# Value products of two attention heads issued alternately, in their own groups of 32 output columns

## The reference, cut to what matters

```python
attn = softmax(q @ k.T * scale + bias)        # per head, 256 x 256
out = jnp.einsum('bqk,bkd->bqd', attn, v)     # per head, 256 x 16: the value product
out = out.reshape(...) @ proj_w + proj_b
```

## Time and profile before

| | us |
|---|---|
| median of 3 runs | 290.22 |
| lowest and highest | 287.61, 291.16 |
| span of the profiled execution, first to last instruction | 287.2 |
| PE busy in it | 241.8 (84%) |
| DVE busy | 106.3 (37%) |
| ACT busy | 78.7 (27%) |
| POOL busy | 25.3 (9%) |

### The profile page before, as it was taken

One profiled execution on the slowest core, in us unless ns is written; L12 is line 12 of the kernel. 1 busy time (PEld: TensorE's weight loads), 2 busy tenths in 40 slices (PEclk: granted clock), 3 DMA queues, 4 the chain that ended last, 5 costly groups with the idle time before them and its releaser, 6 DMA issues.

```text
span 287.2 us, 3244 instructions
## 1 busy us (share of the span) xinstructions
PE 241.8 (84%) x1255; PEld 149.7 (52%) x1266; DVE 106.3 (37%) x262; ACT 78.7 (27%) x156; POOL 25.3 (9%) x45
## 2 busy tenths in 40 slices
PE   7856069999899579999989874999999877499995
PEld 2754046555357256655466443665564762375552
DVE  4566034324638133424311522321125651334222
ACT  2581003432030002342252200224321470023431
POOL 7510812601000000000000000000000000000000
PEclk9975557999999955999999996589999977658999
DMA  6999959409003900000000093000000089200000
GB/s 171 236 153 133 123 139 308 69 3 110 2 1 51 113 0 0 2 0 2 0 0 0 3 124 40 0 0 2 0 0 2 27 109 118 21 0 0 0 3 27
DMA packets 10574, 15.06 MB, mean 52 GB/s; under 512 B 2912, under 2 KB 7296, under 8 KB 10528
## 3 DMA queue, kind: packets, MB, share of 16 engines
q1 hardware_dynamic: 7472, 12.63, 28.0%
q0 software_dynamic: 3088, 2.24, 6.3%
HBM read 8.30 MB, written 0.20 MB: 30 GB/s over the span
## 4 chain that ended last, share of the span: by engine, by line
PE 63%; DMA 15%; DVE 7%; ACT 7%; issue 5%; SPq 2%; DVEq 0%; ACTq 0%
PE PC L940 15%; DMA QS<-RL 9%; PE RING L922 8%; PE RING L879 8%; PE RING L923 6%; DMA QS<-QL 4%; PE PB L960 4%; PE RING L824 4%; PE PC L951 2%; DMA RELT<-in_relt 2%; PE PC L865 2%; PE RING L1111 2%; PE PA L1117 2%; PE PC L943 2%; PE PB L824 1%
## 5 line engine op out<-in xcount | busy, mean ns | idle before, releaser
L738 DVE TENSOR_REDUCE NM<-RING 128x2 fp32r<-128x512 f32 (+1 forms) x48 | 30.8, 658 | 73.9 <-PE RING L879 73.5
L879 PE MATMUL RING<-KS,QS 128*128 128x256 f32 (+1 forms) x96 | 28.4, 404 | 28.2 <-DMA QS<-RL 17.4
L824 PE MATMUL RING<-WARM 128*128 128x512 bf16 x195 | 50.0, 401 | 2.3 <-POOL WARM L343 1.3
L940 PE MATMUL PC<-PR,VX 128*32 128x256 f32 x192 | 47.6, 395 | 0.0
L506 ACT ACTIVATE PR<-RING 128x512 f32<-128x512 f32 x48 | 28.6, 595 | 43.0 <-PE RING L923 42.5
L879 PEld LDWEIGHTS RING<-KS,QS 128*128 128x128 f32 x96 | 20.6, 268 | 36.2 <-issue 33.5
L922 PE MATMUL RING<-QS,KS 128*128 128x256 f32 x96 | 34.3, 374 | 0.3
L824 PEld LDWEIGHTS RING<-WARM 128*128 128x128 bf16 x206 | 20.9, 104 | 25.5 <-issue 4.9
L923 PE MATMUL RING<-MT,SELM 128*128 128x256 f32 (+1 forms) x96 | 30.4, 332 | 0.0
L922 PEld LDWEIGHTS RING<-QS,KS 128*128 128x128 f32 x96 | 20.3, 212 | 16.1 <-issue 10.6
L940 PEld LDWEIGHTS PC<-PR,VX 128*32 128x32 f32 x192 | 16.5, 111 | 17.3 <-issue 3.2
(11 more groups left out here) (153 smaller groups left out, 262.8 us busy)
## 6 DMA issues: line engine op xcount, KB each, us to landing
KS<-KH SPq DMA_DIRECT2D x8, 192.0 KB, 6.8
WQKV<-in_w SPq DMA_DIRECT2D x2, 576.0 KB, 7.2
WO<-in_wo SPq DMA_DIRECT2D x4, 288.0 KB, 9.1
W<-in_ff SPq DMA_DIRECT2D x2, 576.0 KB, 7.6
WQKV<-in_w SPq DMA_DIRECT2D x2, 432.0 KB, 6.6
KS<-in_hot POOLq DMA_DIRECT2D x1, 768.0 KB, 15.4
QS<-QHL SPq DMA_DIRECT2D x2, 384.0 KB, 11.4
KS<-KL SPq DMA_DIRECT2D x4, 192.0 KB, 8.6
```

Source lines behind the costliest of these rows:

```text
L738: V.tensor_reduce(NM[g % 2][:, :, h % GH], slot("m", l, h)[:, 0:2 * n_keys].rearrange("p (q k) -> p q k", q=2), AX.X, ALU.max, negate=True ...
L824: M(bank, WARM[:, 0:P], WARM[:, :], start=True, stop=True)
L879: ins = M(s[:, q * n_keys:(q + 1) * n_keys], QS[l % 2][:, h, q * P:(q + 1) * P], KS[:, h, keys], start=True, stop=True)
L940: ins = M(dst, VX[:, k, h, :], PR[:, h % NPR, k * T:(k + 1) * T], start=(k == 0), stop=(k == 1 and l != 2))
```

## The change

`values` takes two heads. It waits for both heads' probabilities and then issues, for each half of the keys, the matmul of the first head and that of the second; the two heads write different groups of 32 partitions of the same PSUM buffer. The loop calls it at odd `h` from 3 on, for heads `h - 3` and `h - 2`, and once at the end for heads 10 and 11. The number of matmuls is the same, and each does the same work. The other lines of the diff remove empty lines, so line numbers are smaller in the changed kernel (L940 is L897, L922 and L923 are L874 and L875, L879 is L831).

```diff
-            def values(l, h):
+            def values(l, first):
 
-                g, j = h // GH, h % GH
-                pe.wait_ge(*upto("probs", l, h + 1))
-                if h == 0:
+                g = first // GH
+                heads = range(first, first + 2)
+                pe.wait_ge(*upto("probs", l, first + 2))
+                if first == 0:
...
-                dst = PC[g % 2][32 * j:32 * j + 32, 0:T]
+                def columns(h):
+                    return PC[g % 2][32 * (h % GH):32 * (h % GH) + 32, 0:T]
+
                 for k in range(2):
-                    ins = M(dst, VX[:, k, h, :], PR[:, h % NPR, k * T:(k + 1) * T], start=(k == 0),
-                            stop=(k == 1 and l != 2))
+                    for h in heads:
+                        ins = M(columns(h), VX[:, k, h, :], PR[:, h % NPR, k * T:(k + 1) * T], start=(k == 0),
+                                stop=(k == 1 and l != 2))
+                        if k == 1 and l != 2:
+                            ins.then_inc(sem("pv"), 1)
                 if l == 2:
-                    ins = M(dst, VR[:, h, :], PG[g % 2][:, :], start=False, stop=True)
-                ins.then_inc(sem("pv"), 1)
+                    for h in heads:
+                        M(columns(h), VR[:, h, :], PG[g % 2][:, :], start=False, stop=True).then_inc(sem("pv"), 1)
...
-                    if h >= 2:
-                        values(l, h - 2)
+                    if h >= 3 and h % 2:
+                        values(l, h - 3)
...
                 values(l, NH - 2)
-                values(l, NH - 1)
                 out_project(l, 0)
```

More of the change, by code:

```diff
@@ L933, in values @@
                         pe.wait_ge(sem("vr"), 1 + 2 * GH)
-                if j == 0 and g >= 2:
+                if first % GH == 0 and g >= 2:
                     pe.wait_ge(*upto("o", l, g - 1))
-                if j == 0 and l == 2:
+                if first % GH == 0 and l == 2:
                     pe.wait_ge(*upto("reg probs", l, g + 1))
-                dst = PC[g % 2][32 * j:32 * j + 32, 0:T]
+                def columns(h):
+                    return PC[g % 2][32 * (h % GH):32 * (h % GH) + 32, 0:T]
                 for k in range(2):
-                    ins = M(dst, VX[:, k, h, :], PR[:, h % NPR, k * T:(k + 1) * T], start=(k == 0),
-                            stop=(k == 1 and l != 2))
+                    for h in heads:
[3 more added lines that the diff above has]
+                            ins.then_inc(sem("pv"), 1)
                 if l == 2:
-                    ins = M(dst, VR[:, h, :], PG[g % 2][:, :], start=False, stop=True)
-                ins.then_inc(sem("pv"), 1)
+                    for h in heads:
+                        M(columns(h), VR[:, h, :], PG[g % 2][:, :], start=False, stop=True).then_inc(sem("pv"), 1)
             def row_sums(l, g):
```

## The result

| | before | changed |
|---|---|---|
| median, us | 289.22 (4 runs) | 269.11 (4 runs) |
| lowest and highest | 287.61, 291.16 | 267.03, 271.20 |
| span of the profiled execution | 287.2 | 269.4 |
| PE busy in it | 241.8 (84%) | 222.9 (83%) |

The ratio is 0.928, 95% interval 0.922 to 0.933: 20 to 21 us faster, inside the range of 261 to 273 us and 2 us above the forecast of 267.0. Medians and low-clock means in this document are over all runs of a kernel, ratios and their intervals leave out runs more than 1.5% above their kernel's fastest. The profiled execution of the changed kernel was the longest of the four (271.2 us), so its trace shows the losses a little large.

The account below looks back on a forecast made before the run. TensorE was taken to bound the attention loop. Gains of 16.4 us (layers 0, 1, 3) and 6.85 (layer 2), 23.2 in total, took the span from 287.2 to 264.0; 3.0 us more gave 267.0, range 261 to 273.

Parts of the forecast that it names:

- TensorE bounds the loop: Attention loop: the other engines wait for TensorE; over two heads, 3.30 us, PE is busy throughout, ACT 1.19 us.
- A pair costs one product: Two value products in different groups of 32 output columns run side by side: 1.00 us, against 0.98 for one.
- the first pair: Start of each loop, heads 0 and 1 moved behind head 3: gain 0.95 us, not 1.6, DVE being late next.
- The beat of two heads: Two heads in mid-loop, layers 0, 1 and 3: 2.14 us instead of 3.30, gain 1.16 us, three times per layer.
- The end of the loop: Scores of head 10 to `out_project`, 4.74 us before: gain 1.0 to 1.2 us, taken as 1.0.
- Layer 2: Six-row value products: two heads take 2.56 us instead of 4.15, the end gains 1.45; whole layer 6.85 us.
- the sum: Gains added over the loops: 5.45 us each in layers 0, 1 and 3, 6.85 in layer 2, total 23.2 us.
- The clock: Rise from 1.2 to 2.4 GHz in every loop: moments shift, no mean change, 1.5 us to either side.
- rival 1: Clock rises one 3.4 us stretch later: 1.7 us lost per layer, 6.8 in all four, 273.8 us; chance 0.10.
- my signs of being wrong: Five steps in a pair, PE waiting for L506 between scores, or a later clock rise behind a loop's start.

Follow-up runs that it names:

- the filler: Changed kernel with three matmuls on zeros per layer where the value product of head 0 had stood, behind `for_maxima(7)`; 265.65 us, ratio 0.918.

## Why the prediction was right, and which term was off

**TensorE bounds the loop: right.** L897 waits 0.0 us, ACT still sits idle 32 us behind the scores.

**A pair costs one product: right.** Forecast 1.00 us, measured 0.98. The evidence for it, heads 9 and 10 of the kernel before, was also enough to say that the alternation isn't what does it; the run without alternation confirms that, and the one with shared columns shows that without the overlap there is no gain. That holds at the full clock: in layers 1 to 3 the first pair still fell into the low clock, and in layer 1 it took 1.85 us (111.01 to 112.86).

**The beat of two heads: right.** 2.14 us forecast and measured. At head 6 (53.29 to 56.07) it is 2.78 us, no wait for ACT.

**The first pair: right in mechanism, right in size in layer 0 alone.** DVE was late next, as said: TensorE stood 0.36 us, where I had 0.5. Scores of head 2 to scores of head 4 took 4.76 us (46.16 to 50.92) against 5.92 (45.86 to 51.78), a gain of 1.16 where 0.95 stood, part of it a clock that rose some 0.6 us sooner behind these scores (at 48.4 against 48.7). I took the same for the other loops, whose timelines had the same shape; there the stretch became 0.45 to 1.18 us longer, by the clock.

**The end of the loop: right.** From the scores of head 10 to `out_project` 3.72 us (58.21 to 61.93) against 4.74, gain 1.02 for a forecast of 1.0. The profile shows the two blocks of the end:

```profile
59.93 2.06 PE L897 MATMUL PC<-PR,VX 128*32 128x256 f32 x16
...
60.30 0.58 ACT L461 ACTIVATE PR<-RING 128x512 f32<-128x512 f32 x1
...
61.93 0.46 PE L919 MATMUL PB<-O,WO 128*96 128x256 f32 x1
```

**Layer 2: right from head 4 on.** Its end took 4.15 us (196.23 to 200.38), as forecast, instead of 5.60, and from head 4 to `out_project` the gain is 6.08 us, where the sum has 5.95. The layer as a whole gave 5.20 for 6.85, by the stretch ahead of head 4.

**The clock: this term was wrong.** I took "no mean change, 1.5 us to either side". It was 10 us more at the low level per run, of 269 (85 against 75). Over the four windows above, 12.4 us more went with a loss of 5.1 us, 0.41 us for each; by that, as an estimate, 10 us cost some 4 us. Adding them to the measured gain, 289.2 - 269.3 (mean of the two medians) = 19.9, gives 24, beside the 23.2 of the sum. The forecast time was close because what is counted in rows was right at the full clock, and rival 1, to which I gave one chance in ten as a case of its own, happened in most loops at about 0.6 of its price of 6.8 us. Its condition was named and its likelihood was too low: I had seen that the change takes 1.3 us of matmuls out of the stretch ahead of the rise, and then called the wait that remained short. The last of my signs of being wrong, a clock that rises later behind a loop's start, was met in every loop.

A part of the closeness was luck: the forecast started from a median of three runs, 290.22, and with the fourth it is 289.22. From there the same gain leads to 266.0, and the miss is 3 us, not 2. One sum was slightly off without effect: a pair at 0.98 instead of 1.00 gives 0.5 us over 24 pairs, not 0.3.

Layer 0 belongs to this too. In the profile of before, its clock was up from 41.9 to 45.3, in that of the changed kernel not. From the loop's start to the scores of head 2, before:

```profile
38.71:45.86 7.15, 7.00 (x28) 4.90 (x29) 4.07 (x7) 1.50 (x4) 2.33 (x2) 0.74 0.93 248
```

And changed:

```profile
36.80:46.16 9.36, 9.33 (x28) 6.47 (x29) 4.06 (x6) 1.50 (x4) 2.33 (x2) 0.50 0.93 245
```

The same instructions took 7.15 and 9.36 us, before anything that the change moves. In these two profiles it nearly cancels, because the changed kernel's loop also began 1.91 us earlier (36.80 against 38.71, both times on a DMA's landing), so that head 2 came at 46.16 against 45.86. This part is no work of the change's order, and single runs of one kernel differ in low-clock time by more: what in the 10 us is such chance, and what is the change, is separated only by the means. Why the filler lowers the low-clock time more than its own 1.3 us of matmuls per loop, and what exactly makes the clock rise, was not settled.

## What to carry to other kernels

Here a value product with 32 output columns was nearly free when its neighbour in the stream used another group of columns: look for a place in the trace where two already meet, and read the price there. Put them next to each other; the order among them doesn't matter. And when a change takes work off TensorE near the start of a phase, count what it leaves standing there: in these runs the clock rose earlier when the start of the loops was denser, and the work taken out there cost some 4 of 23 us through the clock. Forecast a gain near such a place at both clocks, not at the full one alone.

## What the runs showed of the hardware that I had not expected

- A stretch in which PE reads as fully busy can sit at 1.2 GHz: 9.33 of 9.36 us busy at 0.50, in the row above. The rows there start up to 0.51 us apart and last 0.58 each, and so count as busy throughout. In the kernel before, the clock even fell, at 45.3, behind a stretch of 3.40 us busy of 3.40.
- Four column groups at once: sixteen fp32 rows of 256 columns in 1.07 us, against 1.05 for four rows.
- With a matmul over 2 rows between those over 128, starts at the low clock were 0.51 us apart, with all of them over 128 rows 0.21; making it 128 rows, in three layers, saved 12.7 us with pairs and 11.6 us without (289.24 to 277.69).
- Twelve matmuls on zeros went with 3.8 us less time and 10 us less at the low clock.
